# Groups 2 and 3 of a grouped convolution on quarters of the TensorE array

## The reference

```python
y = conv1d(x, weight, kernel 9, pad 4, 4 groups of 8 channels) + ctx[:, :, None] + bias   # ctx = cond @ c_weight.T
xq = fake_quant(y, per token);  wq = fake_quant(w, per row)      # 8 bit: scale = max|.| / 127, round
gate = xq @ wq_gate.T ; up = xq @ wq_up.T                        # 512 -> 1376
h = silu(gate) * up
out = x + fake_quant(h) @ fake_quant(w_down).T                   # 1376 -> 512
```

## Time and profile before

| | |
|---|---|
| time, median of 3 runs | 282.3 us (282.22 to 282.36) |
| profiled execution, first to last instruction | 280.7 us |
| PE busy | 98% |
| DVE busy | 87% |
| POOL busy | 74% |
| ACT busy | 70% |
| matmul records of line 1207 | 576 of 1862; half of them are groups 2 and 3 |

### The profile page before, as it was taken

One profiled execution on the slowest core, in us unless ns is written; L12 is line 12 of the kernel. 1 busy time (PEld: TensorE's weight loads), 2 busy tenths in 40 slices (PEclk: granted clock), 3 DMA queues, 4 the chain that ended last, 5 costly groups with the idle time before them and its releaser, 6 DMA issues.

```text
span 280.7 us, 5318 instructions
## 1 busy us (share of the span) xinstructions
PE 275.1 (98%) x1862; PEld 153.6 (55%) x1862; DVE 243.5 (87%) x411; ACT 196.4 (70%) x237; POOL 207.4 (74%) x215
## 2 busy tenths in 40 slices
PE   8989999999999999999999999999999999999995
PEld 5978754454564464644444745744444444444443
DVE  0999999999999989799888679789988889888973
ACT  2269999989688886666888836726788886666820
POOL 1478999998969786866888836946778888667732
PEclk9999999999999999999999999999999999999999
DMA  7999923686929999646599992425456763334265
GB/s 268 406 420 419 377 69 71 129 200 171 223 61 221 249 212 238 190 126 187 145 244 296 218 271 77 128 53 128 126 156 163 151 176 98 94 88 124 51 142 187
DMA packets 81721, 51.62 MB, mean 184 GB/s; under 512 B 69664, under 2 KB 70560, under 8 KB 81568
## 3 DMA queue, kind: packets, MB, share of 16 engines
q1 hardware_dynamic: 81264, 50.84, 66.5%
q10 hardware_dynamic: 432, 0.46, 0.5%
HBM read 25.99 MB, written 8.39 MB: 122 GB/s over the span
## 4 chain that ended last, share of the span: by engine, by line
PE 85%; DMA 6%; DVE 4%; SPq 3%; issue 1%
PE bank L1305 52%; PE bank L1329 26%; PE bank L1207 6%; DMA h_mem<-w_gate_up 6%; DVE d_max L855 2%; SPq L352 1%; DVE gu_max L838 1%; SPq L340 1%; PE bank L1344 1%; DVE sg_mem L910 0%; PE bank L1231 0%; SPq L343 0%; DVE sg_mem L989 0%; SPq L329 0%; DVE gu_scale L845 0%
## 5 line engine op out<-in xcount | busy, mean ns | idle before, releaser
L1305 PE MATMUL bank<-wgu_t,xq_mem 128*128 128x512 bf16 (+1 forms) x768 | 154.8, 357 | 0.0
L544 POOL TENSOR_TENSOR sg_mem<-sg_mem,gu_scale_row 128x512 f32<-128x512 f32 (+1 forms) x96 | 110.9, 1162 | 36.3 <-ACT sg_mem L702 36.2
L1305 PEld LDWEIGHTS bank<-wgu_t,xq_mem 128*128 128x128 bf16 x768 | 73.7, 98 | 73.2 <-DVE h_mem L923 1.6
L702 ACT ACTIVATE sg_mem<-sg_mem,x_scale 128x512 f32<-128x512 f32 (+1 forms) x96 | 62.7, 672 | 30.0 <-DVE sg_mem L910 29.5
L1329 PE MATMUL bank<-wd_t,hq_mem 128*128 128x512 bf16 (+1 forms) x341 | 78.2, 379 | 0.0
L923 DVE SCALAR_TENSOR_TENSOR h_mem<-bank,x_scale,sg_mem 128x512 f32<-128x512 f32 (+1 forms) x96 | 65.7, 691 | 8.9 <-POOL sg_mem L544 8.2
L910 DVE TENSOR_TENSOR sg_mem<-bank,gu_scale_row 128x512 f32<-128x512 f32 (+1 forms) x96 | 59.7, 626 | 9.4 <-PE bank L1305 9.2
L707 ACT ACTIVATE h_mem<-h_mem,h_inv 128x1376 f32<-128x1376 f32 (+1 forms) x32 | 45.3, 1419 | 28.2 <-DVE h_inv L831 28.2
L1329 PEld LDWEIGHTS bank<-wd_t,hq_mem 128*128 128x128 bf16 (+1 forms) x341 | 33.4, 98 | 39.6
L928 DVE TENSOR_REDUCE h_max<-h_mem 128x1 f32<-128x1376 f32 x31 | 48.8, 1576 | 0.0
L715 ACT ACTIVATE hq_mem<-h_mem 128x1376 bf16<-128x1376 f32 (+1 forms) x32 | 42.0, 1314 | 0.2
(11 more groups left out here) (71 smaller groups left out, 175.2 us busy)
## 6 DMA issues: line engine op xcount, KB each, us to landing
xo_mem<-x SPq DMA_DIRECT2D x24, 256.0 KB, 3.0
out<-xo_mem SPq DMA_DIRECT2D x24, 256.0 KB, 2.2
hq_mem<-w_gate_up SPq DMA_DIRECT2D x7, 512.0 KB, 10.9
slab_taps<-x_slabs SPq DMA_DIRECT2D x6, 512.0 KB, 5.5
slab<-x_slabs SPq DMA_DIRECT2D x6, 512.0 KB, 8.7
slab_taps<-w_down SPq DMA_DIRECT2D x3, 688.0 KB, 14.2
h_mem<-w_gate_up SPq DMA_DIRECT2D x4, 512.0 KB, 15.8
slab_taps<-x SPq DMA_DIRECT2D x1, 2048.0 KB, 9.8
```

Source lines behind the costliest of these rows:

```text
L544: pool.tensor_tensor(s, s, gu_scale_row[:, 1, at:at + n], ALU.mult).then_inc(silu_scaled, 1)
L702: act.activation(s, s, ACT.Silu, scale=x_scale_of(i)).then_inc(silu_done, 1)
L1305: last = pe.matmul(bank[n % 2][:, 0:cols], xq_t[:, g, k, P * c:P * (c + 1)], wgu_t[:, m, k, at:at + cols], start=(k == 0), stop=(k == KT - 1))
```

## The change

`conv_quad(tile)` takes the place of the pairs of groups 2 and 3. It does four spans side by side, one on each quarter of the array's rows. A quarter holds 8 input channels x 4 positions as its 32 rows, so a span has 18 blocks instead of 9, and the moving band has 8 x 12 = 96 columns (64 and 32 in the two blocks at either end). The stationary operand is 32 rows x 128 columns. Quads stand in tiles 9 and 11 (group 2) and 17 and 19 (group 3), each in place of `down`, which moves behind the tile's last `gate_or_up`. The pair at tile 6 and the one at tile 7 go. Span 16 moves from ACT and POOL to DVE. The data in memory is laid out for it (`x_quads`, `quad_taps`); a piece is half of a quad's 18 blocks, 576 KB, and both pieces are waited for before the quad starts.

```diff
-        PAIRS_AT = {7: 9, 9: 10, 11: 11}
-        FOURS_AT = {17: 3 * PAIRS, 19: 3 * PAIRS + 2}
+        FOURS_AT = {9: 2 * PAIRS, 11: 2 * PAIRS + 2, 17: 3 * PAIRS, 19: 3 * PAIRS + 2}
...
         def conv_bank(q):
-            return banks[(6, 7, 4, 5)[q % 4] if q < FRONT or q >= 3 * SPANS else (6, 7)[q % 2]]
+            return banks[(6, 7, 4, 5)[q % 4] if q < FRONT or q >= PAIR_GROUPS * SPANS else (6, 7)[q % 2]]
...
-        BY_ACT = [2, 4, 5] + list(range(8, 18)) + list(range(19, 32, 2))
+        BY_ACT = [2, 4, 5] + list(range(8, 16)) + list(range(17, 32, 2))
...
+            def load_quad_piece(k):
                 g, i = divmod(k, PAIRS)
...
+                first, end = QUAD_PIECES[i % 2]
+                words = slice(N * (QUAD_BLOCKS * (i // 2) + first), N * (QUAD_BLOCKS * (i // 2) + end))
+                sp.dma_start(slab_words[g % 2][:, words], x_quads[g - PAIR_GROUPS, :, words]).then_inc(pair_in[k], 16)
...
-            shift_span(16)
-            shift_span(17)
...
-            copy_span(16)
-            copy_span(17)
...
-            fold_y(17)
...
+            def conv_quad(tile):
+                k = FOURS_AT[tile]
+                g, i = divmod(k, PAIRS)
+                spans = range(2 * k, 2 * k + 4)
+                for piece in range(2):
+                    pe.wait_ge(pair_in[k + piece], 16)
+                if k == PAIR_GROUPS * PAIRS:
+                    pe.wait_ge(quad_taps_in, 16)
+                for q in spans[0:2]:
+                    conv_bank_free(pe, conv_before(q))
+
+                pe.wait_ge(down_scaled, tile - LAG)
+                for b in range(QUAD_BLOCKS):
+                    at = QUARTER_STEP * b - 2 * PAD
+                    lo, hi = max(at, 0), min(at + QUAD_REACH, SPAN)
+                    for q, quarter in zip(spans, QUARTERS):
+                        out_span = conv_bank(q)[:, :].rearrange("p (c l) -> p c l", c=CI)
+                        last = pe.matmul(out_span[:, :, lo:hi], quads[g % 2][quarter, i // 2, b, :],
+                                         quad_rows[quarter, g - PAIR_GROUPS, :, lo - at:hi - at],
+                                         start=(b == 0), stop=(b == QUAD_BLOCKS - 1), skip_group_check=True)
+                        if b == QUAD_BLOCKS - 1:
+                            last.then_inc(conv_done, 1)
...
-            conv_pair(8)
...
                 if i in FOURS_AT:
-                    conv_pair(FOURS_AT[i])
-                    conv_pair(FOURS_AT[i] + 1)
+                    conv_quad(i)
                 else:
                     down(i - LAG)
-                if i in PAIRS_AT:
-                    conv_pair(PAIRS_AT[i])
```

More of the change, by code:

```diff
@@ L31, with adaln_ffn @@
 SECOND = 5
-def adaln_ffn(nc, x, x_first, x_slabs, cond_ctx_bias, taps, w_gate_up, w_down, out):
+QUARTER_STEP = 4
+def adaln_ffn(nc, x, x_first, x_slabs, x_quads, cond_ctx_bias, taps, quad_taps, w_gate_up, w_down, out):
     N, C, L = x.shape
@@ L58, in adaln_ffn @@
     assert BLOCKS == NEW + 1
-    assert x_slabs.shape == (GROUPS, P, SLAB) and x_first.shape == (P, BAND + FIRST * N)
-    assert taps.shape == (P, (GROUPS - 1) * BAND)
+    PAIR_GROUPS = 2
+    QUAD_GROUPS = GROUPS - PAIR_GROUPS
+    QUADS = SPANS // 4
+    QUAD_BLOCKS = (SPAN + 2 * PAD) // QUARTER_STEP
+    QUAD_REACH = QUARTER_STEP + 2 * PAD
+    QUAD_BAND = CI * QUAD_REACH
+    QUAD_SLAB = QUADS * QUAD_BLOCKS * N
+    QUARTERS = tuple(slice(P // 4 * r, P // 4 * (r + 1)) for r in range(4))
+    QUAD_PIECES = ((0, QUAD_BLOCKS // 2), (QUAD_BLOCKS // 2, QUAD_BLOCKS))
+    assert x_slabs.shape == (PAIR_GROUPS, P, SLAB) and x_first.shape == (P, BAND + FIRST * N)
+    assert x_quads.shape == (QUAD_GROUPS, P, QUAD_SLAB)
+    assert taps.shape == (P, (PAIR_GROUPS - 1) * BAND) and quad_taps.shape == (P, QUAD_GROUPS * QUAD_BAND)
     TPG = CI * P
@@ L90, in adaln_ffn @@
         sg_mem = sb("sg_mem", [P, SG_BUFS * INTER])
-        slab0_taps0 = sb("slab0_taps0", [P, BAND + SLAB])
-        slab1 = sb("slab1", [P, SLAB])
+        slab0_taps0 = sb("slab0_taps0", [P, BAND + QUAD_SLAB])
+        slab1 = sb("slab1", [P, QUAD_SLAB])
         y_mem = sb("y_mem", [P, CI * L])
@@ L97, in adaln_ffn @@
         xo_mem = sb("xo_mem", [P, XO_BUFS * L])
-        band_rest = sb("band_rest", [P, (GROUPS - 1) * BAND])
+        band_rest = sb("band_rest", [P, (PAIR_GROUPS - 1) * BAND])
+        quad_bands = sb("quad_bands", [P, QUAD_GROUPS * QUAD_BAND])
         ident = sb("ident", [P, P])
@@ L123, in adaln_ffn @@
         slab_words = [slab0, slab1[:, :]]
-        slabs = [words.rearrange("p (b n) -> p b n", n=N) for words in slab_words]
+        slabs = [words[:, 0:SLAB].rearrange("p (b n) -> p b n", n=N) for words in slab_words]
+        quads = [words.rearrange("p (j b n) -> p j b n", j=QUADS, n=N) for words in slab_words]
+        quad_rows = quad_bands[:, :].rearrange("p (g c o) -> p g c o", g=QUAD_GROUPS, c=CI)
         def pair_blocks(k):
@@ L189, in conv_bank @@
         def conv_bank(q):
-            return banks[(6, 7, 4, 5)[q % 4] if q < FRONT or q >= 3 * SPANS else (6, 7)[q % 2]]
+            return banks[(6, 7, 4, 5)[q % 4] if q < FRONT or q >= PAIR_GROUPS * SPANS else (6, 7)[q % 2]]
         def conv_before(q):
-            return q - 2 if FRONT + 2 <= q < 3 * SPANS + 2 else q - 4
-        BY_ACT = [2, 4, 5] + list(range(8, 18)) + list(range(19, 32, 2))
+            return q - 2 if FRONT + 2 <= q < PAIR_GROUPS * SPANS + 2 else q - 4
+        BY_ACT = [2, 4, 5] + list(range(8, 16)) + list(range(17, 32, 2))
         BY_DVE = [q for q in range(SLOTS) if q not in BY_ACT]
@@ L215, in adaln_ffn @@
         taps_1_in = sem("taps_1_in")
-        taps_rest_in = sem("taps_rest_in")
+        quad_taps_in = sem("quad_taps_in")
         y_part_ready = sem("y_part_ready")
@@ L298, in spans_at @@
         def spans_at(i, by):
-            first = 2 * FOURS_AT.get(i, PAIRS_AT.get(i, 0))
-            n = 4 if i in FOURS_AT else 2 if i in PAIRS_AT else 0
-            return [q for q in range(first, first + n) if q in by]
+            return [q for q in range(2 * FOURS_AT[i], 2 * FOURS_AT[i] + 4) if q in by] if i in FOURS_AT else []
         def down_bank_of(i):
@@ L331, in load_pair, with load_taps_of_group_1 @@
             def load_pair(k):
+                g = k // PAIRS
+                words = new_words(k)
+                sp.dma_start(slab_words[g % 2][:, words], x_slabs[g, :, words]).then_inc(pair_in[k], 16)
+            def load_taps_of_group_1():
+                sp.dma_start(band_rest[:, 0:BAND], taps[:, 0:BAND]).then_inc(taps_1_in, 16)
+            def load_quad_piece(k):
                 g, i = divmod(k, PAIRS)
@@ L336, in load_pair, with load_quad_taps @@
                 elif i == 0 and g == 3:
[L338 to L346, removed]
+                    sp.wait_ge(conv_done, PAIR_GROUPS * SPANS)
+                first, end = QUAD_PIECES[i % 2]
+                words = slice(N * (QUAD_BLOCKS * (i // 2) + first), N * (QUAD_BLOCKS * (i // 2) + end))
+                sp.dma_start(slab_words[g % 2][:, words], x_quads[g - PAIR_GROUPS, :, words]).then_inc(pair_in[k], 16)
+            def load_quad_taps():
+                sp.dma_start(quad_bands[:, :], quad_taps).then_inc(quad_taps_in, 16)
             def load_w(j):
@@ L442, in _ @@
             load_w_down(3)
-            load_other_taps()
+            load_quad_taps()
             turn_yq(2)
@@ L451, in _ @@
             turn_w_down(2)
-            load_pair(8)
+            load_quad_piece(8)
             turn_hq(0)
@@ L456, in _ @@
             turn_hq(1)
-            load_pair(9)
+            load_quad_piece(9)
             turn_hq(2)
@@ L472, in _ @@
                 if i in LOADS_AT:
-                    load_pair(LOADS_AT[i])
+                    load_quad_piece(LOADS_AT[i])
                 if i == 15:
@@ L1193, in conv_pair @@
                         conv_bank_free(pe, conv_before(q))
-                if k - 1 in FOURS_AT.values():
-                    tile = next(i for i, first in FOURS_AT.items() if first == k - 1)
-                    pe.wait_ge(down_scaled, tile - LAG)
                 for b in range(BLOCKS):
@@ L1478 @@
     x_slabs = np.ascontiguousarray(x_slabs.reshape(2, n, c // ci, ci, blocks, STEP).transpose(2, 0, 3, 5, 4, 1)
-                                   .reshape(c // ci, 128, blocks * n))
+                                   .reshape(c // ci, 128, blocks * n)[:2])
+    quad_blocks = (span + 2 * PAD) // QUARTER_STEP
+    x_quads = np.stack([x_wide[:, 2 * ci:, half * h + span * k:half * h + span * k + QUARTER_STEP * quad_blocks]
+                        for k in range(half // span) for h in range(2)])
+    x_quads = np.ascontiguousarray(x_quads.reshape(2, 4, n, c // ci - 2, ci, quad_blocks, QUARTER_STEP)
+                                   .transpose(3, 1, 4, 6, 0, 5, 2).reshape(c // ci - 2, 128, -1))
     weight = np.asarray(L0_cond_weight).reshape(c // ci, ci, ci, 2 * PAD + 1).transpose(2, 0, 1, 3)
@@ L1485 @@
     taps = taps.reshape(128, c // ci, -1)
```

(8 more changed lines are left out.)

2 lines of the change are left out of this document (removed).

## The result

The changed kernel takes 286.2 us (286.07 to 286.37, 3 runs) against 282.3: ratio 1.0139, 95% interval [1.0125, 1.0153]. It is slower by 3.9 us, and 286.2 was forecast. The profiled execution's span, first to last instruction, went from 280.7 to 284.4 us. The forecast took the time around the span as 1.6 us, the difference of a median and one profiled span. Where the record has both for one run, it is 1.8 us, before and after (282.38 and 280.6, 286.23 and 284.4), so it did stay the same.

A forecast was written before the change was run, and what follows sets the result against it. PE was taken to set the end, with DVE, ACT and POOL close behind at tiles 6 and 7; -0.35 + 4.04 + 0.2 = +3.9 us on 282.3 gave 286.2 us, range 283.8 to 290.5.

The forecast's parts named there:

- part 1: Convolution on PE: a quad takes 4.17 us, the same as two pairs; 0.27 us less PE work in all.
- the short records: Line 1207: matmuls with 64 moving columns save 9 of 54 ns, so the weight load paces a half, at 0.112 us.
- Rival (a): Quads run at the pace of moving data, four times 1.27 us less, kernel 281.1 us; chance 0.11.
- rival (b): Quads held by PE's instruction rate, up to 7.5 us more, kernel 293.7, halfway 290; chance 0.13.
- part 2: Tile 6: without its pair PE waits for DVE; of 2.16 us 0.15 come forward, 2.0 become a stall.
- part 3: Tile 7: without its pair up 7.2 starts 0.5 us earlier; by tile 9 both pairs have brought 0.35.
- part 4: Tiles 9 and 11: PE stays the bound, quads replace pairs, 4.04 us later, plus 0.2 for DVE.
- The DVE backlog behind four spans: After tile 11: the 24 matmuls of one later tile take 0.17 us more, 0.2 with hundredths on the way.
- The sum: Whole kernel: -0.35 + 4.04 + 0.2 = +3.9 us on the span, so 286.2 us.
- Rival (c): No stalls at tiles 6 and 7, the pairs' 4.31 us come off in full: 282.2 us, no change; chance 0.06.
- Rival (d): PE's clock falls in the new stalls of 2.0 and 1.7 us: 287.2 us; counted within the forecast's 0.70.

The follow-up runs named there:

- the third: Changed kernel with quads of 32 stationary and 32 moving columns, count of instructions kept, most of the convolution of groups 2 and 3 left out: 283.3 us.
- The cut pair: Kernel before with the pair of tile 6 cut to one of its nine blocks: 282.7 us against 282.5, ratio 1.0004.
- the order on halves: Kernel before with the changed kernel's order, two adjacent pairs on halves in place of each quad: 286.8 us against 282.5, ratio 1.0149.

## Why the prediction was right

**The quad, part 1.** 4.17 us forecast, 4.15 in all four. The reading that loads of weights pace a half, from the short records, held for quarters. Three eighths of the moving columns left 4.15, half the stationary ones gave 2.91. Rival (a), quads at the pace of moving data, and rival (b), held by instructions, fell with these two and the third. Rival (a)'s price was wrong too: the forecast took 1.27 us a quad, 5.1 in all, off the kernel, for 281.1. The run with quads of 2.91 us gave 283.5: as far as one run shows, such quads would still have left the kernel slower than before, and a quad of 3.2 us would not have turned the verdict. The step that fails there is that PE alone bounds the tiles of the quads.

**The pair at tile 6, part 2.** Forecast: 2.0 of 2.16 us turn into a stall, 0.15 comes forward. (The forecast's opening has the distance at this pair as nearly all the pair. By its rows the distance is short, 63.50 - 63.22 = 0.28 us; it is the stall left by the pair that is nearly all of it, as part 2 says.) The stall is 1.93 us, and the piece behind it starts 0.42 earlier, 0.16 without the 0.26 from before tile 0. The cut pair says the same in its starts, 0.16.

**The pair at tile 7, part 3.** Forecast: up 7.2 comes 0.5 forward, up 9.0 0.35. Without the 0.26 these are 0.50 and 0.35. The stall was put at 1.7 and is 1.49 in the profile: by then PE's lead had shrunk from 0.42 to 0.15, at a `down` at 72.42 us whose weight loads waited for a DMA.

**Tiles 9 and 11, part 4.** Forecast 2 x 2.02; the starts behind them step by 2.01 and 2.00. The DVE backlog behind four spans was put at 0.2 us and is 0.40: 0.04 in each of tiles 10 and 12, and 0.15 or so in both 13 and 15, where I had counted one such tile. This is the one term of the sum that was off; it is twice what was forecast. That it turned up in the order on halves as well shows that it goes with the place.

**The sum.** -0.26 (before tile 0) - 0.35 + 4.01 + 0.40 - 0.04 (two quads of group 3, 0.02 each) = 3.76 us, the distance of all pieces from tile 21 on. The span grew by 3.7, the times by 3.9; the 0.2 missed in the backlog and the 0.26 from before tile 0 about cancel in the span. Without what came before tile 0 the change costs 4.02 us, where 3.9 was forecast; that 286.2 was met to the tenth is luck.

**Rival (c)**, that no stall appears, is out by the two waits. **Rival (d)**: the granted clock stayed at 1.00 over the stretch from 58 to 95 us, with stalls of 1.93 and 1.49 us in it (busy us and instructions of each engine, then clock, DMA share, GB/s):

```profile
58.00:95.00 37.00, 33.48 (x170) 15.29 (x168) 33.28 (x57) 29.05 (x33) 28.99 (x29) 1.00 0.81 185
```

## What to carry to other kernels

An engine that is busy all the time, and alone in the chain of waits, isn't the bound at every place: compare the start of each of its instructions with the end of what frees its buffer, and that distance is the most that can be won by taking out work ahead of it. Where it is short beside a piece of other work that stands there, nearly all that work is free. Before moving such work, ask which stall it fills and what the new place costs; the sum of busy time says nothing of it. This holds for work that only gets shorter as well: it gives back no more than the engines next behind allow. For small matmuls on parts of the array, find out which of load, moving data and issue paces them from records in which only one of these differs.

## What was not expected of the hardware

With 32 moving columns in each block, TensorE's clock fell from 2.4 GHz to 1.2 in parts of the run. The windows of that kernel (busy us and instructions of each engine, then the granted clock, DMA share and GB/s):

```profile
94.89:99.04 4.15, 4.15 (x145) 4.11 (x146) 3.15 (x5) 3.28 (x4) 4.07 (x5) 1.00 0.80 197
113.24:117.82 4.58, 4.58 (x145) 4.52 (x146) 3.70 (x7) 2.89 (x3) 3.64 (x3) 0.89 0.81 195
...
161.60:166.71 5.11, 5.11 (x146) 5.04 (x146) 3.14 (x5) 3.28 (x4) 4.94 (x5) 0.79 1.07 204
168.22:170.88 2.66, 2.66 (x8) 1.21 (x8) 2.33 (x4) 1.83 (x2) 2.28 (x3) 0.50 1.03 232
```

A mean between 1.00 and 0.50 is a stretch with both. PE was busy without a gap in these quads, at the same count of instructions as in the changed kernel, whose clock stayed at 1.00; only the moving columns had become fewer. In two of four quads the clock gave way, and for the bf16 pieces soon after one of them it was at half. The kernel took 291.1 us, 5 more than the changed one, which moves 2.7 times as many columns in its quads. The third kernel of that set, which moves 32 columns as well but has quads of 1.7 us, kept 1.00. In the changed kernel PE stood idle for 1.93 and 1.49 us with the clock at 1.00 before and after; here it fell while PE was busy throughout. This is one run, and two of its four quads kept the full clock, so what lowers it stays open.
